# An attention kernel whose last query block is divided by its sums at the end, with the steps of a slot in another order

## What is computed

```python
g = silu(ffn(xn))                        # 512 -> 2048 -> 512, relu squared, five spiking steps
attn = softmax(q @ k.T * 512 ** -0.5)    # 16 heads of 32 features, 1024 x 1024 a head and batch
attn = attn + bias_table[i - j + 511]    # 1023 rows; an index past the end takes the last row
s = layernorm(attn @ v)                  # with gamma and beta
out = x + s * g
```

## Time and profile before

| | |
|---|---|
| median of 3 runs | 3528.83 us (3526.05 to 3529.10) |
| span of the profiled execution | 3528.6 us |
| busy, share of the span | PE 97%, ACT 74%, DVE 71%, POOL 49% |
| granted TensorE clock, mean | 0.996 |

### The profile page before, as it was taken

One profiled execution on the slowest core, in us unless ns is written; L12 is line 12 of the kernel. 1 busy time (PEld: TensorE's weight loads), 2 busy tenths in 40 slices (PEclk: granted clock), 3 DMA queues, 4 the chain that ended last, 5 costly groups with the idle time before them and its releaser, 6 DMA issues.

```text
span 3528.6 us, 55344 instructions
## 1 busy us (share of the span) xinstructions
PE 3421.4 (97%) x19961; PEld 1441.3 (41%) x19964; DVE 2506.6 (71%) x4051; ACT 2624.2 (74%) x3898; POOL 1720.5 (49%) x998
## 2 busy tenths in 40 slices
PE   7999999999999999999999999999999999999996
PEld 3444444444444444433433433433433433433431
DVE  5555555555555555777888888888888888888887
ACT  6433333333333335999999999999999999999997
POOL 0012222111111123899666666666666666666672
PEclk9999999999999999999999999999999999999999
DMA  5122322333222222222322322322322322322322
...
DMA packets 238752, 312.35 MB, mean 89 GB/s; under 512 B 96624, under 2 KB 132208, under 8 KB 238480
## 3 DMA queue, kind: packets, MB, share of 16 engines
...
...
## 4 chain that ended last, share of the span: by engine, by line
ACT 33%; PE 11%; issue 10%; DVE 4%; SPq 1%; DMA 1%; ACTq 0%; POOL 0%; DVEq 0%; POOLq 0%
ACT recurrence_or_probs L1457 17%; ACT s_sb L1464 16%; PE misc L1331 3%; PE acc L1406 3%; PE s_ps L1386 3%; PE s_ps L1372 2%; DVE s_sb L1533 2%; DMA xT<-xnT 1%; SPq L322 1%; DVE gate_or_tokens L1662 0%; PE misc L1313 0%; DVE outT L1553 0%; DVE x_or_queries L1570 0%; DVE gate_or_tokens L1665 0%; PE s_ps L1331 0%
## 5 line engine op out<-in xcount | busy, mean ns | idle before, releaser
L1739 POOL TENSOR_TENSOR recurrence_or_probs<-recurrence_or_probs,toep 128x512 f32<-128x512 f32 (+1 forms) x375 | 1288.5, 3457 | 366.5 <-ACT recurrence_or_probs L1457 366.2
L1533 DVE TENSOR_SCALAR_CACHE_REDUCE s_sb<-s_ps 128x1024 f32<-128x1024 f32 x998 | 1213.7, 1220 | 353.8 <-PE s_ps L1372 325.7
L1464 ACT ACTIVATE s_sb<-s_sb,nmax 128x1024 f32<-128x1024 f32 x998 | 1167.0, 1169 | 9.8 <-DVE s_sb L1533 9.5
L1457 ACT ACTIVATE recurrence_or_probs<-s_ps 128x1024 f32<-128x1024 f32 x1024 | 1060.1, 1036 | 7.7 <-PE s_ps L1386 7.5
L559 PE MATMUL ps_fc<-xnT_part,w_fc 128*128 128x512 f16 x3072 | 707.2, 380 | 4.5 <-DVE w_fc L817 4.5
L574 PE MATMUL ps_y<-w_pr,hid_part 128*128 128x512 f16 x3072 | 706.2, 380 | 3.6 <-issue 2.6
L740 ACT ACTIVATE relu<-ps_fc 128x512 f32<-128x512 f32 x256 | 152.7, 597 | 626.9 <-PE ps_fc L559 626.9
L130 POOL TENSOR_TENSOR recurrence_or_probs<-gate_or_tokens,beta_row 128x512 f32<-128x512 f32 x60 | 89.9, 1499 | 1035.3 <-DVE gate_or_tokens L185 1031.7
L929 DVE TENSOR_TENSOR hid<-relu 128x512 f32<-128x512 f32 x256 | 210.3, 822 | 510.9 <-ACT relu L740 510.9
L1406 PE MATMUL acc<-recurrence_or_probs,val 128*32 128x512 f32 x4096 | 545.2, 604 | 2.2 <-DVE recurrence_or_probs L1649 1.5
L559 PEld LDWEIGHTS ps_fc<-xnT_part,w_fc 128*128 128x128 f16 x3072 | 300.6, 98 | 369.3 <-issue 7.8
(11 more groups left out here) (180 smaller groups left out, 2685.1 us busy)
## 6 DMA issues: line engine op xcount, KB each, us to landing
...
```

Source lines behind the costliest of these rows:

```text
L1457: nc.scalar.activation(prob[:, k % PROBS, 2 * second:2 * second + 2, :].rearrange("p j n -> p (j n)"), s_ps[:, item_buffer(pair_item(m)), ...
L1464: nc.scalar.activation(s_sb[:, i % 4, :], s_sb[:, i % 4, :], ACT.Exp, bias=nmax[:, par, j, st:st + 1], scale=-1.0, accum_out=den[:, par, j ...
L1533: nc.vector.tensor_scalar(s_sb[:, i % 4, :], s_ps[:, item_buffer(tile_item(n)), :], -1.0, None, ALU.mult, ALU.min, accum_out=nmax[:, par, ...
L1739: nc.gpsimd.tensor_tensor(tile, tile, toep[:, par, :, at:at + width], ALU.add).then_inc(biased, 1)
```

## The change

**The last query block (block 7, `LATE`)** of each head gets no sum before its exp. Its tile is still computed and its maximum taken (now with a plain maximum that writes no copy), but ScalarE's exp with sum is left out for these 4 of 32 tiles of a group (`SUMMED`). Its logarithm stays 0, so its probabilities are exp(score - maximum), undivided. GpSimd adds these up over the 8 key blocks (`sum_late`, 7 additions of 512 elements a partition), TensorE sums over the partitions (`late_denominators`, 4 matmuls), and VectorE multiplies by the reciprocal in `copy_acc`. The bias of this block can't be added to undivided probabilities; it isn't constant for one key block only, which TensorE weighs apart (`late_bias`, 4 matmuls of the bias with the values) and VectorE adds at the end.

**Far bias.** The table is stored less its far row, so the far part is the sum of all values of the batch. Token sums are taken in `feed_forward` (`sum_tokens`, two reductions a chunk on VectorE) and projected once in slot 0; `sum_values` goes.

**Order.** Tiles come in `TILE_ORDER`, in which block 7's stand at 6, 15, 21 and 28, thus in half-steps 12, 21, 27 and, of the next slot, 2. Key blocks come in `KEY_ORDER`, wide and narrow bias by turns. The value projections move to half-steps 1, 2, 6 and 7, the query and key projections are cut in 3 parts of 4 matmuls, rows and transposes move by one.

```diff
+TILE_ORDER = ((0, 0), (0, 1), (0, 2), (0, 3), (1, 0), (1, 1), (0, 7), (1, 2), (1, 3), (2, 0), (2, 1), (2, 2), (2, 3), (3, 0), (3, 1), (1, 7),
+              (3, 2), (3, 3), (0, 4), (0, 5), (0, 6), (2, 7), (1, 4), (1, 5), (1, 6), (2, 4), (2, 5), (2, 6), (3, 7), (3, 4), (3, 5), (3, 6))
+LATE = 7
...
-VALUES = {0: (0, 0), 2: (0, 1), 4: (1, 0), 6: (1, 1)}
-SUM_VALUES, ROWS_1, ROWS_0, OUT_1, OUT_0 = 8, 10, 27, 28, 30
+VALUES = {1: (0, 0), 2: (0, 1), 6: (1, 0), 7: (1, 1)}
+QUERY_KEYS = {12 + 4 * u + i: (u, i) for u in range(4) for i in range(3)}
+LATE_BIAS = 8
+FAR_VALUES, ROWS_1, ROWS_0, OUT_1, OUT_0 = 4, 10, 28, 29, 30
+KEY_ORDER = ((4, 0, 5, 1, 6, 2, 7, 3), (0, 4, 1, 5, 2, 3, 6, 7))
+COPY_1, COPY_0 = 6, 22
-LOG_0 = 11
+LOG_0 = 12
+COPIES = 3
...
+            return min(LATE * P - 512 if k >= 8 else 512, (key_block(k) + 1) * P - k // 8 * 512)
...
             def weigh(b, hg, k):
-                if bias_width(k) > 0:
...
+                pe.wait_ge(biased, pool_count(g, k))
...
+            def late_denominators(g):
+                take_misc()
+                pe.wait_ge(biased, pool_count(g, SLOT_STEPS - 1))
+                for j in range(HG):
+                    last = nc.tensor.matmul(misc[j * HD:(j + 1) * HD, :P], ones_col[:], late_sum[:, j, :], start=True, stop=True)
+                last.then_inc(den_ps, 1)
+
+            def late_bias(s):
+                take_misc()
+                for j in range(HG):
+                    last = nc.tensor.matmul(misc[j * HD:(j + 1) * HD, :P], val[:, s.par, LATE, j * HD:(j + 1) * HD],
+                                            toep[:, s.par, j, TW - P:], start=True, stop=True)
+                last.then_inc(late_ps, 1)
...
                     if second and (s.main if k >= WEIGH_LAG else s.prev):
-                        weigh(*last_weighed(b, hg, h))
+                        for done in weighed_at(b, hg, k):
+                            weigh(*done)
+                        if k == 2:
+                            late_denominators(s.g - 1)
...
             def exp_sum(G, par, i):
+                if not SUMMED[i]:
+                    return
...
             def row_max(G, par, i):
+                if not SUMMED[i]:
+                    nc.vector.tensor_reduce(nmax[:, par, j, st:st + 1], s_ps[:, item_buffer(tile_item(n)), :], AX, ALU.max,
+                                            negate=True).then_inc(max_done, 1)
+                    return
...
+            def copy_acc(g, half):
+                if half == 0:
+                    nc.vector.tensor_scalar(outT[:, 0, :], acc[:], from_far, None, ALU.add).then_inc(acc_read, 1)
+                    return
+                dve.wait_ge(den_ps, g + 1)
+                nc.vector.reciprocal(late_scale[:], misc[:, :P]).then_inc(den_read, 1)
+                nc.vector.tensor_scalar(outT[:, 1, :late.start], acc[:, :late.start], from_far, None, ALU.add)
+                dve.wait_ge(den_read, g + 1)
+                nc.vector.tensor_tensor(outT[:, 1, late], acc[:, late], late_scale[:], ALU.mult).then_inc(acc_read, 1)
+                nc.vector.tensor_tensor(outT[:, 1, late], outT[:, 1, late], late_out[:], ALU.add).then_inc(out_made, 1)
...
+            def sum_late(b, hg, k):
+                if k < 9:
+                    return
+                pool.wait_ge(p_done, g * 32 + k * 2 + 2)
+                before_it = late_sum[:] if k > 9 else prob[:, 8 % PROBS, :, late]
+                nc.gpsimd.tensor_tensor(late_sum[:], before_it, prob[:, k % PROBS, :, late], ALU.add).then_inc(biased, 1)
...
                     if s.main and k >= 1:
                         add_bias(b, hg, k - 1)
+                        sum_late(b, hg, k - 1)
...
+            def sum_tokens(c, par, part):
+                nc.vector.tensor_reduce(spiking.token_sums[:, c * 2 + part, :], xnT[:, par, part], AX,
+                                        ALU.add).then_inc(tokens_summed, 1)
...
+            def sum_values():
+                for hg in range(HG):
+                    for n, (k, a, bb) in enumerate((k, a, bb) for k in range(EB) for a, bb in TERMS):
+                        last = nc.tensor.matmul(misc[:, hg * NB:(hg + 1) * NB], w["v"][:, bb, k, hg * P:(hg + 1) * P],
+                                                batch_parts[:, a, :, k], start=(n == 0), stop=(n == 11))
```

More of the change, by code:

```diff
@@ L276, in subtracted @@
         pool.wait_ge(self.ln_done, n + 1)
+        if half == 1:
+            pool.wait_ge(self.max_done, G * 32 + 32)
         wait(pool, self.rows_ps, n - 1)
@@ L346, in feed_forward @@
         rows, known = d["tableT"].shape
-        table = sb("table", [rows, d["table_ext"].shape[1]], F32)
+        table = hidden.rearrange("p i a n -> p (i a n)")[:rows, :d["table_ext"].shape[1]]
+        far_row = sb("far_row", [rows, 1], F32)
         y = spiking.y
@@ L593, in first_tile @@
             def first_tile(i):
-                j, st = first.of_tile(i)
-                if i < 16 and i % 4 == 0:
+                j, st = TILE_ORDER[i]
+                if i in FIRST_OF_HEAD:
                     pe.wait_ge(first.stacked[j], 96)
@@ L1199, in prelude_bank, with weighed_at @@
             return (misc, 0, spiking.xT_first) if n % 2 else (s_ps[:, RING - 1, :BANK], 1, spiking.xT_first)
-        def last_weighed(b, hg, h):
-            k = h // 2 - WEIGH_LAG
-            return (b, hg, k) if k >= 0 else (*before(b, hg), SLOT_STEPS + k)
+        def weighed_at(b, hg, k):
+            ready = (k - WEIGH_LAG,)
+            return [(b, hg, i) if i >= 0 else (*before(b, hg), SLOT_STEPS + i) for i in ready]
         @block.sync
@@ L1328, in project_qk @@
                 terms = [(k, a, bb) for k in range(EB) for a, bb in TERMS]
-                for n in range(part * 6, part * 6 + 6):
+                for n in range(part * 4, part * 4 + 4):
                     k, a, bb = terms[n]
@@ L1356, in transpose_out @@
                 pe.wait_ge(acc_read, g * 2 + half + 1)
+                if half == 1:
+                    pe.wait_ge(out_made, g + 1)
                 for q in range(4):
@@ L1378, in score_pair @@
                 x = pair_item(s.g * 32 + 2 * k + second)
-                half, tb = k // 8, k % 8
-                if tb == 0 and second == 0:
+                half, tb = k // 8, key_block(k)
+                if k % 8 == 0 and second == 0:
                     pe.wait_ge(rows_loaded[half], s.g * 64 + 64)
@@ L1548, in copy_acc, with split_sums @@
-            def copy_acc(g, par, half):
+            def split_sums():
+                sums = spiking.token_sums.rearrange("p (b i) k -> p b k i", b=NB)
+                nc.vector.tensor_reduce(batch_sums[:], sums, AX, ALU.add).then_inc(sums_split, 1)
+                dve.wait_ge(sums_split, 1)
+                nc.vector.tensor_copy(batch_parts[:, 0], batch_sums[:]).then_inc(sums_split, 1)
+                dve.wait_ge(sums_split, 2)
+                nc.vector.tensor_tensor(batch_parts[:, 1], batch_sums[:], batch_parts[:, 0], ALU.subtract).then_inc(sums_split, 1)
@@ L1733, in add_bias @@
                     return
[L1734 removed]
+                at = bias_from(k)
                 if k == 0:
```

244 lines of the change are left out of this document (157 added, 87 removed).

## The result

The changed kernel takes 3677.36 us (median of 4, 3671.71 to 3679.72), the kernel before 3527.94 beside it: a ratio of 1.0421, 95% interval 1.0407 to 1.0436. The forecast was 3578 in 3515 to 3612. Slower was right; the loss is 149 us where 50 was forecast. The profiled execution has a span of 3676.6 us against 3528.6, and that is where its lines are from.

The account below looks back on a forecast made before the run. ScalarE sets the pace, TensorE 2% behind; after the change TensorE's order makes ScalarE wait. From 3528.6: slots 4 to 30 +32, slots 0 to 3 +5, gate +11, rest +5, less 4 for merged waits: 3578, range 3515 to 3612.

Parts of the forecast that it names:

- ScalarE is the bound, TensorE 2% behind, little can be had: Steady slots before the change: ScalarE sets the pace, and TensorE can at once give back what is taken from it.
- The rule for the lead: Half-step sum of how early TensorE has each pair ready for ScalarE, capped by three buffers: waits of 5.5 us a slot.
- ScalarE's own 61.5: ScalarE's work per slot after the change: 28 x 2.035 + 4 x 0.97 + 0.65 = 61.5 us.
- `copy_acc` gets some 0.7 more at half-step 6, where it has time: VectorE's work at half-step 6 grows by some 0.7 us, where it has time.
- ScalarE's 0.57 of waits for it I keep: ScalarE's waits for VectorE in slots 4 to 30 stay 0.57 us a slot (0 to 1.2).
- GpSimd: hidden: GpSimd has 53 us of work in a slot of 67; its longest queue runs under 6 us late, hidden before the weighing.
- The gate, 11 (4 to 16), with 5 of the slots: Weighings wait for GpSimd around slots 1 and 2: +11 us (4 to 16); slots 0 to 3 add 4 x 1.2 = +5.
- Late bias and denominators 0.45 each, a maximum alone 1.22: TensorE's two new groups of 4 matmuls take 0.45 us each; VectorE's plain maximum over 1024 columns takes about 1.22.
- The last slot: VectorE's late addition waits longer for subtraction rows, 2 us, plus 1 for the longer end of `copy_acc`.
- GpSimd deciding every slot: Rival: slower strided additions or the weighing's new wait cost one more us in each slot, 3610 or more; chance 0.12.
- ScalarE keeps the bound: Rival: 31 x 4.26 = 132 us off, 3400 with the gate, needing TensorE under 61.5 a slot; chance 0.03.

Follow-up runs that it names:

- the add is mended: Changed kernel with VectorE's product written back to PSUM, so the last addition reads one input there and not both in SBUF: 3651.92 us.
- its run: Changed kernel with the last addition reading PSUM, and a plain copy in place of the reciprocal (last block not normalised): 3643.47 us.
- all three edits: Changed kernel with the last addition reading PSUM, value projections at half-steps 0, 2, 6 and 8, and GpSimd's late sums left out: 3544.11 us.

## Why the prediction was right in direction and wrong in size

**ScalarE is the bound, TensorE 2% behind, little can be had**: right. Cutting the sums with nothing else changed gave 21 us, where ScalarE was relieved of 3.8 a slot, some 118 in all.

**The rule for the lead:** right in its main places and nearly in their sizes. In the 25 steady slots of the kernel after, ScalarE's mean waits for a pair stand behind these half-steps: 13: 1.05 (forecast 1.11), 3: 0.94 (1.00), 22: 0.67 (0.77), 29: 0.67 (0.69), 1: 0.40 (0.52), 25: 0.18 (0.12). The two of 0.16 behind 17 and 21 aren't there, nor those behind 2 and 7; at 7 VectorE's wait of 1.55 takes the place, and once the add is mended TensorE's 1.00 is there (forecast 0.77). In sum 4.15 for 5.5. But the prediction worked its rule wrongly in four places: the lead into half-step 7 is 0.37 + 2.04 - 2.22 = 0.19 and not 0.51, a wait of 1.09, and at 17, 23 and 25 the rule gives 0.43, 0.25 and 0.50 where 0.16, 0 and 0.12 stand. Done right its waits are 6.7 and not 5.5. Against the 4.15 measured, and 4.86 with the add mended, the rule counts too much, and the slips hid part of that.

**ScalarE's own 61.5:** measured 62.85. The forecast took back-to-back starts for all of its instructions. With some ten waits a slot, each costs 0.12 to 0.15 of lost overlap on top. It is luck that the two errors cancel: 61.5 + 5.5 = 67.0 against 62.85 + 4.15 = 67.0.

**"`copy_acc` gets some 0.7 more at half-step 6, where it has time", and "ScalarE's 0.57 of waits for it I keep":** this is the step that failed. Four instructions take from 2200.86 to 2205.65, 4.8 us, where 0.7 more than one was counted. The price came from instructions that read PSUM; the one added instruction whose inputs both lie in SBUF runs beside a GpSimd that is inside additions of 4.56 us. The prediction took each engine's durations as its own. The 1.55 in half-step 7 is this addition's; the 2.3 in half-steps 21 to 24 are old instructions of VectorE, which the forecast left as they were. ScalarE's waits for VectorE are 3.89 instead of 0.57: (3.89 - 0.57) x 27 = 90, and in the ordinary slots the forecast, at +32, is 89 short of the +121. Taking both causes away gives 83 us (3677.36 to 3594.48), 17 of them in slots 0 to 3, since TensorE's waits take some of the place. With the add mended and the late sums gone VectorE's waits are 0.98, and the slot 68.44 against the forecast 67.5; the reciprocal (0.36 a slot by its run) is in the difference.

**"GpSimd: hidden"** in ordinary slots: right of its queue, no weighing waits long for it; wrong of its effect. It costs not by being late but by holding VectorE, 1.77 us a slot.

**The gate, 11 (4 to 16), with 5 of the slots:** 16 forecast for slots 0 to 3, 18.7 measured: -2.1, +9.3, +9.1 and +2.4. The size is near, the cause isn't: it isn't the weighings that wait, but the rows to subtract, which stand behind the queue on GpSimd. TensorE's timeline:

```profile
1539.23 0.58 PE L317 MATMUL misc<-identh,subT 128*128 128x128 f16 x4 [5.90 <-POOL subT L304]
...
1613.93 0.59 PE L317 MATMUL misc<-identh,subT 128*128 128x128 f16 x4 [4.16 <-POOL subT L304]
```

5.90 and 4.16 in slots 1 and 2, each with 6.8 us of half clock around its end; the run without late sums has neither, and its slots 0 to 3 are 14.4 us shorter.

**Late bias and denominators 0.45 each, a maximum alone 1.22:** nearly right, 0.36 and 0.33 from start to start, and 1220 ns in the lines by form. Ahead of slot 0 nothing was forecast, and 1.8 came. **The last slot** had +3, and +6.3 came; TensorE's clock was at half for 6.8 us from 3613 on, and what that cost is open.

**The rivals.** GpSimd deciding every slot (0.12, "3610 or more") came nearest in size, by another mechanism than the two it names. That ScalarE keeps the bound and its saving is had is refuted by the run with cut sums. By the Trainium skill (Perfetto Trace Analysis, Identifying the Most-Contended Engine) the engine with the highest occupancy is to be optimised first; here another stood 2% behind, and 21 us were to be had.

What stays open: which of its waits make the version with all three edits 0.3 us a slot slower than the kernel before; how much of the excess over a sum of parts is the clock; what makes the last slot 6.3 us longer; and whether another order of the steps would let the saved sums count.
